# Two fused layers on one core: the first layer's casts of gate weights moved behind the last queries, value sums in front of low parts, and routing cut into five parts

## The reference, cut to what matters

```python
qkv = silu(xn @ qkv_w.T)                       # 32 heads: q, k, v of 128 features each
attn = decayed, causal (q @ k.T) @ v           # per head, without a softmax
xf = attn * rsqrt(mean(attn * attn) + EPS)     # over all heads
y = (sigmoid(xn @ gate_w.T) * norm_w * xf) @ out_w.T
scores = softmax(xn @ router_w + router_b) + router_bias
# two of four groups of experts, then two of the experts left; ffn = shared expert
# + sum over the two chosen experts of score * expert(xn)
x = x + y + ffn
```

## Time and profile before

| what | value |
|---|---|
| median of 3 runs | 2634.18 us (2630.57 to 2636.35) |
| the profiled execution's own time | 2634.02 us |
| its span, first to last instruction | 2632.2 us |
| mean granted TensorE clock over the span | 0.989 |
| TensorE busy | 2492.2 us, 95% |
| VectorE (DVE), ScalarE (ACT), GpSimd (POOL) busy | 1590.3, 1359.3, 1584.9 us |

### The profile page before, as it was taken

How to read it: one execution, slowest core, us unless ns; L and a number is a source line. 1 busy time by engine, 2 the same in 40 slices (tenths; PEclk the granted TensorE clock), 3 DMA queues, 4 the chain that set the end, 5 groups by cost and what they waited for, 6 DMA issues and landing times.

```text
span 2632.2 us, 42349 instructions
## 1 busy us (share of the span) xinstructions
PE 2492.2 (95%) x13850; PEld 2132.6 (81%) x13850; DVE 1590.3 (60%) x2449; ACT 1359.3 (52%) x2694; POOL 1584.9 (60%) x1523
## 2 busy tenths in 40 slices
PE   7999999999999999989999999999999999959999
PEld 6878888888878888777878888888878878847777
DVE  6555555646565647875465555646564788864553
ACT  5545555555555555544555455555555557733332
POOL 4756666666666754756676667767776678731210
PEclk9999999999999999989999999999999999989999
DMA  4211111111111113211111111111111078931110
GB/s 151 83 41 41 60 45 43 52 44 52 36 52 44 48 45 105 73 45 45 45 51 36 60 49 39 52 44 52 36 52 45 31 245 299 303 110 45 33 32 32
DMA packets 89052, 183.87 MB, mean 70 GB/s; under 512 B 12610, under 2 KB 38866, under 8 KB 88966
## 3 DMA queue, kind: packets, MB, share of 16 engines
q1 hardware_dynamic: 80422, 165.94, 19.2%
q0 software_dynamic: 8544, 16.82, 2.2%
HBM read 163.81 MB, written 26.79 MB: 72 GB/s over the span
## 4 chain that ended last, share of the span: by engine, by line
PE 50%; issue 17%; POOL 14%; DVE 10%; ACT 5%; SPq 2%; DMA 1%; POOLq 0%; DVEq 0%; ACTq 0%
PE bank L95 16%; PE bank L96 15%; PE bank L97 15%; POOL wl L1958 5%; POOL ol L1970 2%; POOL sqacc L1976 2%; POOL w_in L511 1%; POOL w_in L513 1%; POOL w_in L515 1%; DVE q_lo L1676 1%; PE bank L1091 1%; DVE ms_lo L1689 1%; PE bank L1118 1%; SPq L2208 1%; ACT wh L1390 1%
## 5 line engine op out<-in xcount | busy, mean ns | idle before, releaser
L1958 POOL TENSOR_TENSOR wl<-w_in,wh 128x512 fp32r<-128x512 f32 x510 | 629.9, 1260 | 344.7 <-ACT wh L1390 339.5
L95 PE MATMUL bank<-xh,wh 128*128 128x512 f32 x1400 | 561.4, 401 | 31.4 <-ACT qT L1360 27.0
L97 PE MATMUL bank<-xh,wl 128*128 128x512 f32 x1400 | 548.6, 392 | 0.0
L95 PEld LDWEIGHTS bank<-xh,wh 128*128 128x128 f32 x1400 | 264.3, 189 | 91.3 <-ACT qT L1360 30.8
L1976 POOL TENSOR_TENSOR sqacc<-sqacc,sq 128x512 f32<-128x512 f32 x128 | 166.6, 1301 | 263.2 <-ACT sq L1375 254.8
L1390 ACT CAST wh<-w_in 128x512 fp32r<-128x512 f32 x502 | 263.8, 564 | 117.0 <-POOL w_in L517 117.0
L96 PE MATMUL bank<-xl_sums,wh 128*128 128x512 f32 x800 | 316.2, 395 | 0.0
L97 PEld LDWEIGHTS bank<-xh,wl 128*128 128x128 f32 x1400 | 263.8, 188 | 59.1
L95 PE MATMUL bank<-wh,xh 128*128 128x256 f32 x912 | 258.6, 284 | 5.8 <-DVE xl L569 3.3
L96 PE MATMUL bank<-wl,xh 128*128 128x256 f32 x912 | 257.9, 283 | 0.0
L1732 DVE TENSOR_TENSOR acc<-bank,acc 128x512 f32<-128x512 f32 x240 | 163.0, 687 | 153.4 <-PE bank L97 152.1
(11 more groups left out here) (373 smaller groups left out, 6419.4 us busy)
## 6 DMA issues: line engine op xcount, KB each, us to landing
w_in<-in_w_pairs_dram SPq DMA_DIRECT2D x100, 512.0 KB, 3.8
o_in<-in_o_pairs_dram SPq DMA_DIRECT2D x32, 512.0 KB, 3.5
eraw<-in_ex_dram SPq DMA_DIRECT2D x31, 513.0 KB
y_slots<-ey SPq DMA_DIRECT2D x31, 512.0 KB
w_in<-in_w_pairs_dram SPq DMA_DIRECT2D x56, 256.0 KB, 3.0
dcur<-in_decay_dram SPq DMA_DIRECT2D x32, 256.0 KB
eraw<-in_ex_dram SPq DMA_DIRECT2D x31, 256.0 KB
out_dram<-acc SPq DMA_DIRECT2D x16, 256.0 KB, 2.0
```

What stands on the lines that cost most here:

```text
L95: pe.matmul(out, wh, mh, start=start and i == 0, stop=False, skip_group_check=True)
L97: ins = pe.matmul(out, wl, mh, start=False, stop=stop and i == n - 1, skip_group_check=True)
L1958: pool.tensor_tensor(wl[:, cols], w_in[:, cols], wh[:, cols].bitcast(F32), ALU.subtract).then_inc(w_lo, 1)
```

## The change

1. ACT, even rounds: the four casts of the gates' weights go from around step a of section 0 to behind `high_kq(u, 3)`. Odd rounds and round 1: all four now stand there together.
2. POOL, even rounds: the sums of the values' weights (`add(r, "v0")`) go in front of the gates' low parts.
3. ACT, round 0: `high_ms`, `high_v` and `high_kq` go in front of the keys' casts (in the second half also in front of `take_v` of pieces 2 and 3).
4. ACT, round 1: the keys' four casts go from steps c and b of section 2 to behind the four `take_v`, one behind each.
5. DVE, second half: `place` is cut into `slots_of_choices` (4 operations, at the end of round 0), `columns` (6, behind `summed(r, 0, "e")` of round 1) and the rest (7 operations, now behind `mask(u, 2)`); `gates_of_choices` goes behind `add_out(u, 1)`, and `summed(r, 1, "e")` in front of `experts_of_tiles`.
6. TensorE, round 1 of the second half: products 7 and 3 of section 1 go in front of `project_out(r, 2)`, and product 4 in front of `project_out(r, 3)`.

No operation is added or taken away.

```diff
-    def place(self, v, slot_of, ready):
+    def slots_of_choices(self, v):
...
         for i, m in enumerate((self.m0, self.m1)):
             c.link(v.tensor_tensor(self.prod, m, self.slot, ALU.mult))
-            c.link(v.tensor_reduce(s[:, i, :], self.prod, AX_X, ALU.add))
...
+            c.link(v.tensor_reduce(self.s[:, i, :], self.prod, AX_X, ALU.add))
...
+    def columns(self, v):
+        self.whole(v, self.column, self.s, 1.0 / P, P, 1.0 - SLOTS)
+
+        self.whole(v, self.tile, self.s, 1.0 / SLOT_T, SLOT_T, 2.0 * (STEP - 1))
+
+    def place(self, v, slot_of, ready):
+        c, s, tile = self.chain, self.s, self.tile
+        self.whole(v, self.wrap, tile, STEP / (2.0 * (STEP - 1) * NTILES), NTILES, -2.0 * NTILES)
+        c.link(v.scalar_tensor_tensor(s, s, float(SLOTS // P), self.column, ALU.mult, ALU.add))
+        c.link(v.tensor_tensor(tile, tile, self.wrap, ALU.add))
         c.link(v.tensor_tensor(s, s, tile, ALU.add))
         v.tensor_copy(slot_of[:], s).then_inc(ready, 1)
         v.wait_ge(ready, 1)
@@ tensor, run
-                        project_out(r, 2)
-                        section(r, 1, 7)
-                        project_out(r, 3)
...
+                        if r.second and last:
+
+                            section(r, 1, 7, 3)
+                            project_out(r, 2)
+                            section(r, 1, 4)
+                            project_out(r, 3)
+                        else:
...
@@ scalar, run
-                    if r.even:
-                        split(r, "g", 0, 1)
                     take(r, 0, "a")
-                    if r.even:
-                        split(r, "g", 2, 3)
...
                         high_kq(u, 3)
-                    if r.second or r.odd:
-                        split(r, "g", 0, 1)
+                    if not r.first and not r.end:
+                        split(r, "g", 0, 1, 2, 3)
                     if not r.first:
                         square(u, 2)
                         high_ms(u, 3)
                         high_v(u, 3, odd)
-                    if r.second or r.odd:
-                        split(r, "g", 2, 3)
...
-                    if r.second or r.odd:
+                    if r.odd:
                         split(r, "k", 0, 1)
...
-                    if r.second or r.odd:
+                    if r.odd:
                         split(r, "k", 2, 3)
                     if r.first:
+                        high_ms(0, 0)
+                        high_v(0, 0, False, taken_n(r, "v", 1))
+                        high_kq(0, 1)
                         if last:
                             take_v(r, 2)
                         split(r, "k", 0, 1)
                         if last:
                             take_v(r, 3)
                         split(r, "k", 2, 3)
-                        high_ms(0, 0)
-                        high_v(0, 0, False, taken_n(r, "v", 3))
-                        high_kq(0, 1)
                     if r.second:
-                        for i in V_ORDER:
+                        for n, i in enumerate(V_ORDER):
                             take_v(r, i)
+                            split(r, "k", n)
@@ vector, run
+                        if last:
+                            router.slots_of_choices(v)
                     else:
...
                         summed(r, 0, "e")
+                        if second and last:
+                            router.columns(v)
                         gated(u, 1)
                         mask_pieces(u, 2)
                         mask(u, 2)
+                        if second and last:
+                            router.place(v, slot_of, v_slots)
...
                         low_v(u, 2, odd)
-                        if second and last:
-                            router.place(v, slot_of, v_slots)
                         add_out(u, 0)
...
+                        add_out(u, 1)
                         if second and last:
                             router.gates_of_choices(v, gate_of)
-                        add_out(u, 1)
-                        if second and last:
+                            summed(r, 1, "e")
                             router.experts_of_tiles(v, expert_of, gates, v_gates)
-                        add_out(u, 2)
-                        summed(r, 1, "e")
+                            add_out(u, 2)
+                        else:
+                            add_out(u, 2)
+                            summed(r, 1, "e")
@@ gpsimd, run
                     add_squares(u, 1)
+                    if r.even:
+                        add(r, "v0")
                     low(r, "g")
                     if r.second:
                         low(r, "v")
-                    if r.even:
-                        add(r, "v0")
```

More of the change, by code:

```diff
@@ L248, in count @@
         self.col = tmp
-    def place(self, v, slot_of, ready):
+    def slots_of_choices(self, v):
         c = self.chain
         shape = "p (i t) -> p i t"
-        s, col, tile, wrap = (x.rearrange("p t g -> p (t g)")[:, i * 2 * NT:(i + 1) * 2 * NT].rearrange(shape, i=2)
-                              for x in (self.gm, self.keep) for i in range(2))
+        self.s, self.column, self.tile, self.wrap = (
+            x.rearrange("p t g -> p (t g)")[:, i * 2 * NT:(i + 1) * 2 * NT].rearrange(shape, i=2)
+            for x in (self.gm, self.keep) for i in range(2))
@@ L255, in place @@
         for i, m in enumerate((self.m0, self.m1)):
             c.link(v.tensor_tensor(self.prod, m, self.slot, ALU.mult))
-            c.link(v.tensor_reduce(s[:, i, :], self.prod, AX_X, ALU.add))
-        def whole(out, val, scale, size, factor):
-            c.link(v.tensor_scalar(out, val, scale, (size - 1) / (2.0 * size), ALU.mult, ALU.subtract))
-            c.link(v.tensor_scalar(out, out, ROUND, None, ALU.add))
-            c.link(v.tensor_scalar(out, out, ROUND, factor, ALU.subtract, ALU.mult))
@@ L265, in place, with whole @@
-        whole(col, s, 1.0 / P, P, 1.0 - SLOTS)
-        whole(tile, s, 1.0 / SLOT_T, SLOT_T, 2.0 * (STEP - 1))
-        whole(wrap, tile, STEP / (2.0 * (STEP - 1) * NTILES), NTILES, -2.0 * NTILES)
-        c.link(v.scalar_tensor_tensor(s, s, float(SLOTS // P), col, ALU.mult, ALU.add))
-        c.link(v.tensor_tensor(tile, tile, wrap, ALU.add))
+            c.link(v.tensor_reduce(self.s[:, i, :], self.prod, AX_X, ALU.add))
+    def whole(self, v, out, val, scale, size, factor):
+        c = self.chain
+        c.link(v.tensor_scalar(out, val, scale, (size - 1) / (2.0 * size), ALU.mult, ALU.subtract))
+        c.link(v.tensor_scalar(out, out, ROUND, None, ALU.add))
+        c.link(v.tensor_scalar(out, out, ROUND, factor, ALU.subtract, ALU.mult))
@@ L1203, in run @@
                         section(r, 1, 2)
-                        project_out(r, 2)
-                        section(r, 1, 7)
-                        project_out(r, 3)
-                        if r.end and last:
-                            gates_by_feature(0)
-                            gates_by_feature(1)
-                        section(r, 1, 3)
-                        if r.end:
-                            values(r, 3)
-                        section(r, 1, 4)
+                        if r.second and last:
[4 more added lines that the diff above has]
+                        else:
+                            project_out(r, 2)
+                            section(r, 1, 7)
+                            project_out(r, 3)
+                            if r.end and last:
+                                gates_by_feature(0)
+                                gates_by_feature(1)
+                            section(r, 1, 3)
+                            if r.end:
+                                values(r, 3)
+                            section(r, 1, 4)
                         if r.end and last:
```

## The result

The changed kernel takes 2563.68 us (median of 4 runs, 2563.58 to 2564.22) against 2632.38 for the kernel before beside it: 0.974 of its time, with a 95% interval of 0.9723 to 0.9758. The profiled executions differ by 70.25 us (2634.02 and 2563.77); 63.9 were forecast.

The account below looks back on a forecast made before the run. TensorE, busy 95% of the span, was taken as the bound, with time lost in waits and low clock. Even rounds 51.8 + round 0 3.1 + routing 11.0 - keys' casts 2.0 = 63.9 us, so 2634.0 becomes 2570.1; range 2556 to 2590.

Parts of the forecast that it names:

- Gates' casts: ACT, even rounds: step a loses the wait in front of it, 4.08 us a round; odd rounds and round 1: 0.
- Values' sums: POOL, even rounds: sums fit in idle time but may push `q_lo`; cost 0.4 us, bounds 1.0 lost to 0.5 gained.
- The rule that spoke against this step: DVE two-input SBUF operations and GpSimd ones reading SBUF exclude each other; taken fully, even rounds win 3.1 us, total 2578.5.
- Round 0: High parts in front of keys' casts: shorter wait for `v_lo` and no low clock behind it, 3.1 us (1.5 to 4.3).
- Routing: Round 1, second half: cut-up routing nearly hides in DVE's gaps, 5.0 us left standing; wins 11.0 us (6 to 14).
- Keys' casts in round 1: ACT: casts between takes and in front of `high_v` cost 1.0 us a half, 2.0 in all (1.0 to 2.6).
- Blocked low parts: Rival: DVE's low parts each wait out a POOL operation, even rounds win 3.1 us; 2579 to 2584; chance 0.22.
- routing stays long: Rival: even rounds as forecast, but routing's lengthened pieces win 4 us instead of 11; 2577; chance 0.12.
- nothing moves: Rival: the stall returns at `scores(u, 3)` as a wait for `q_lo`; within 5 us of 2634; chance 0.03.
- POOL's slower queue: Rival: sums for `v1` end too late for ACT's cast in front of t5, section 2; about 2650; chance 0.03.
- all hidden: Rival: even rounds reach 35.11 us, routing wins 14, round 0 4.3, casts cost 1.5; 2560; chance 0.09.
- signs of being wrong: `scores(u, 3)` waits over 1 us (even rounds); ACT waits for `v0`/`v1` sums; DVE waits over 8 us (second half's round 1).

## Why the prediction was right, step by step

The time, 2563.68 us, lies 6.4 below the 2570.1 of the sum, at the lower edge of the forecast (2563 to 2576). Of these, 1.4 us come from parts that no edit touches, so they are luck; the even rounds make up most of the rest.

**Gates' casts.** Right as put: the wait for step a is gone, the casts end in ACT's idle time, the odd rounds keep their 35.11 us.

**Values' sums.** "I take half a sum, 0.4 us" is the step that was mis-sized, and most of the miss: fourteen whole even rounds win 56.6 us where 51.8 were put, which is 4.8 of the 6.4 us. None of the 0.4 came in the round shown, as the last sum ends 0.2 us before `q_lo` begins; it still runs when `k_lo` begins, but `k_lo` takes no more than its 0.43 us. The bounds (a loss of 1.0, a gain of 0.5) hold it. That they had to go first, as I argued, is shown by the sums put back; that it is the second half that needs it, 1.24 us a pair for 0.18, as POOL sends tokens there, I had not seen. My own expectation of that run, no difference, was worse than the prediction's sentence.

The rule that spoke against this step did hold in the durations: `ms_lo` and `v_odd_lo`, begun beside a sum, end 0.54 and 0.29 us after that sum has ended. In the Trainium skill, page "SBUF — State Buffer", section "Who interferes with whom", the later of two such operations is blocked until the earlier has finished; this trace agrees with it within 0.14 us, as `ms_lo` alone takes 0.68 us. Here that costs nothing, as DVE still waits 0.66 us for `project_out` behind the two.

**Round 0.** 3.1 forecast, 3.4 measured; the wait is 1.11 us (1.1 forecast), the clock 1.00. Undone, it costs 4.5 in the first half and 2.2 in the second. Of the 0.9 us to be given back in front of steps ab and t5, one wait of 0.19 us shows, for the sum that needs t5.

**Routing.** 11.0 forecast, 11.4 measured in the window and 10.8 over the whole round, with 4.6 us of excess left in the window for 5.0. That the sum came out is partly luck, as the parts were put wrongly: TensorE's order got a share and has none, nothing is left behind the experts ahead of product 5, and the remainder is five small waits from 0.23 to 0.98 us in front of and at `scores(u, 3)`.

**Keys' casts in round 1.** The 2.0 us forecast are there to the tenth (0.51 and 0.48 in each half), shown by taking them out again. Left out was the clock behind the longer wait (last section). The sentence that the low parts and the sending have slack, "0, or 1 us once", holds in this place, but not far behind it: with the casts behind `high_kq` the first even round of the second half took 7 us longer.

**Rivals.** Blocked low parts, routing stays long, nothing moves and POOL's slower queue did not come; all hidden came nearest, in the even rounds. Of the signs of being wrong, one came once: ACT waits 1.94 us for sums of `v1`, in the first even round of the second half, and TensorE doesn't wait behind it. POOL's queue was the right thing to fear: with the casts or the sums a little later, the cast of `v1` in front of t5 does cost time by the rival's chain, 0.2 to 4 us a round where the rival had 6.

## What to carry to other kernels

A wait that returns every second round is best read against the round without it: the difference of two windows of equal work gave 4.08 us, and 4.09 came in the window, 4.04 on average over whole rounds. Before work is put later into an idle stretch of a helper, follow that helper's queue to the next consumer: here the same delay was free in odd rounds and cost 33 us in all when the even rounds and the rounds 1 had to give it too. And test the parts of a change one by one even when it wins: one of these costs 2 us, one does nothing. A sum that meets the total to the tenth is no proof that its terms are right.

## What the runs showed of the hardware that was not expected

Behind the same wait of 1.75 us, in the same place, TensorE's granted clock stayed at 1.00 in some executions and fell to 0.71 in the mean of the next 5.9 us in others, which mixes the levels of 1.2 and 2.4 GHz. In the two profiles of the changed kernel this is 1.2 us of difference up to the next odd round (139.24 and 140.42 us from round 1's start). A wait near that length thus has no fixed price, and half a microsecond less, 1.24, left the clock at 1.00 in all 12 cases seen.

The kernel before shows it too. Behind its waits of 1.5 to 1.8 us for step a, the prediction had read that the clock stays at 1.00, and so it did in the round of the earlier trace rows; in 2 of the 14 even rounds it fell. One of them, from the end of that wait on:

```profile
407.14:410.54 3.40, 3.40 (x12) 2.88 (x13) 0.49 (x1) 3.40 (x8) 2.07 (x2) 0.64 0.37 128
```

That round's window is no longer for it (39.20 us for 39.19): two waits of 0.23 and 0.49 us, which follow in the round of the earlier trace rows, are missing there. Here a stretch of low clock in front of other waits cost nothing.
